# The loads and stores of 97 or 98 rows cut into 96 rows and a rest, in a graph kernel on one core

## The chip, the cores and the metric

The kernel runs on one core of a Trainium2 chip. A core has four computing engines, TensorE (PE), VectorE (DVE), ScalarE (ACT) and GpSimd (POOL), and SyncE (SP), which here issues nearly all direct transfers. The transfers run on 16 DMA engines that the core's queues share. The metric is the device time of one execution in microseconds (us); lower is better.

## The reference

There are 6250 nodes with 64 features each, and 200,000 edges sorted by their receiving node. Two layers follow each other.

```python
# layer 0: an average over the edges, weighed by the edges' own attributes
zmax = max(x, axis=-1)
q = 0.95 * zmax[src] * e[:, 1] + e[:, 0]
z_new = 0.2 * x + 0.8 * segment_sum(q, dst) / (segment_sum(e[:, 1], dst) + 1e-6)
x = layernorm(x + where(deg > 0, z_new, x))
# layer 1: four heads of attention over the same edges
s = einsum('hef,hef->eh', Q[:, dst], K[:, src]) * 64 ** -0.5
alpha = segment_softmax(s, dst)
agg = segment_sum(alpha * V[:, src], dst)      # mean over the heads
x = layernorm(x + (x + nan_to_num(agg) @ Wout))
```

## The kernel before, in words

The program has a preparation, a first edge stage (layer 0), a node update, a second edge stage (layer 1) and an end. The change touches transfers of the preparation and one store between the two edge stages.

**Preparation.** The lists `src` and `dst` are brought into SBUF as rows of RE = 2048 edges, one row on each partition: 97 full rows and a last one of 1344 edges, TP_ = 98 rows in all. SP waits for `s_init` (VectorE has cleared the last rows of `src_raw` and `dst_raw`) and then issues, in this order, `src_raw` (L287, L288), `dst_raw` (L289, L290), the node features `x` (L292 for 48 blocks of 128 nodes, L293 for the last 106 nodes) and six transfers of weights (L295 to L298). An engine issues in its program's order, so a transfer that SP can't hand over yet holds all behind it.

VectorE waits for `src_raw` (`s_sall`) and makes of it the codes `row_a`, `row_b` and `row_q` (L558 to L568), and the high part of each index (L562), which ScalarE casts (L985). SP stores the three rows of codes to `codes_dram` (L302, with two rows more at the end, L303). VectorE then waits for `dst_raw` (`s_dall`) and makes the receivers' place relative to the lowest of their chunk (L572 to L582, after which `s_rel` is set), and the table of visits (L586 to L605, then `s_vst`). SP stores that table and loads it back as one row (L310 to L315, `s_vld`).

TensorE turns four weights (L1181, once all weights are there, `s_w`), which ScalarE copies (L978 to L982) ahead of its cast of the high parts (L985). TensorE then turns the high parts (L1194), ScalarE copies them out of PSUM (L992), and only then, with `s_rel` set too, TensorE turns the relative places with the same line L1194 and the same four banks. VectorE clears `code_t` (L615) only after that (`s_relT`), and goes on with the table of node maxima (L627 to L633), the window numbers (L638 to L642) and the number of passes (L704, which needs `s_vld`), and sets `s_max`. That releases SP, PE, ACT and POOL into the first edge stage.

GpSimd makes its constants, clears the sums (`acc`, L428), waits for the stored codes (`s_coded`) and for `s_rel`, and clears `present` (L432).

**First edge stage.** 196 steps of 1024 edges: SP loads the edge attributes (L327) and the codes (L320), the other engines work in a pipeline.

**Between the stages.** ScalarE permutes the receivers (`dst_perm`, L1029, `s_dstt`), SP stores them to `dst_turned` (L373) and waits for that store (`s_dsts`) and then for the last sums (`s_all1`). The node update follows on the other engines.

**Second edge stage.** GpSimd gathers the updated nodes of 391 chunks with indirect transfers (L518); the other engines work on each chunk.

Of the kernel before, what the change touches and what calls it, by code (L numbers as in the profile page):

```python
# [14 lines left out]
CPP = 4  # L15
CH = P * CPP
# [6 lines left out]
def gnn_resnorm_kernel(nc, x, src, dst, edge, Wq, Wk, Wv, Wout, out):  # L23
    N, D = x.shape
    E = src.shape[0]
# [12 lines left out]
    FULL = E // CH  # L38
    SJ = 2 * CPP
    SC = P * SJ  # L40
    NS = -(-E // SC)
# [5 lines left out]
    W = 24  # L47
# [3 lines left out]
    SB = 3  # L51
    U2 = 48
    H2 = 7
    NCH = FULL + 1
    NC = -(-NCH // S2) * S2
    NBL = NC // S2
    EPAD = NC * CH
    TP_ = NC // CPP
    assert NS % UN == 0 and UN % S1 == 0 and UN % (4 * RQ) == 0 and 0 < TAIL <= P and (E - (NS - 1) * SC) % CPP == 0 and NC % CPP == 0
    assert NS * SC == EPAD and 2 * TP_ == NS and (NCH - H2) % U2 == 0 and NBL > SB and E - FULL * CH > 0 and (E - FULL * CH) % CPP == 0 and 2 * W <= D and NS % 4 == 0  # L60
    UG = -(-NB // 4)
    assert NB % 4 == 1
    LAST = N - (NB - 1) * P
# [2 lines left out]
    with ctx:  # L66
# [6 lines left out]
        def sem(name):  # L73
            return ctx.enter_context(nc.semaphore(name))


        dst_turned = nc.dram_tensor("dst_turned", [EPAD], F32, kind="Internal").ap()
        codes_dram = nc.dram_tensor("codes_dram", [3, EPAD + 4 * SC], BF16, kind="Internal").ap()
# [10 lines left out]
        RE = CPP * CH  # L89
        src_raw = big[0:TP_, t0:t0 + RE].bitcast(I32)  # L90
# [40 lines left out]
        dst_raw = O[0:TP_, 4 * HB:4 * HB + RE].bitcast(I32)  # L131
# [9 lines left out]
        dst_perm = big[0:TP_, t1 + RE:t1 + 2 * RE]  # L141
# [67 lines left out]
        s_dstt, s_dsts, s_x, s_w, s_dall, s_sall, s_vst, s_vld, s_codes, s_coded = (  # L209
            sem(n) for n in ("dst_turned", "dst_stored", "x_loaded", "w_loaded", "dst_all_loaded", "src_all_loaded",  # L210
                             "visits_stored", "visits_loaded", "codes_made", "codes_stored"))
# [62 lines left out]
        def blocks(g):  # L274
            return min(TB, NB - TB * g)
# [7 lines left out]
        def _(sp):  # L283

            LR = E - (TP_ - 1) * RE
            sp.wait_ge(s_init, 1)
            sp.dma_start(src_raw[0:TP_ - 1, :], src[0:(TP_ - 1) * RE].rearrange("(a b) -> a b", b=RE)).then_inc(s_sall, 16)  # L287
            sp.dma_start(src_raw[TP_ - 1:TP_, 0:LR], src[(TP_ - 1) * RE:E].rearrange("(a b) -> a b", b=LR)).then_inc(s_sall, 16)  # L288
            sp.dma_start(dst_raw[0:TP_ - 1, :], dst[0:(TP_ - 1) * RE].rearrange("(a b) -> a b", b=RE)).then_inc(s_dall, 16)  # L289
            sp.dma_start(dst_raw[TP_ - 1:TP_, 0:LR], dst[(TP_ - 1) * RE:E].rearrange("(a b) -> a b", b=LR)).then_inc(s_dall, 16)  # L290
            sp.wait_ge(s_x, 16)
            sp.dma_start(x1v[:, 0:NB - 1, :], x[0:(NB - 1) * P, :].rearrange("(b p) d -> p b d", p=P)).then_inc(s_x, 16)  # L292
            sp.dma_start(x1v[0:LAST, NB - 1, :], x[(NB - 1) * P:N, :]).then_inc(s_x, 16)  # L293
# [5 lines left out]

            def put_codes(r, t, n):  # L300
                sp.wait_ge(s_codes, n)
                sp.dma_start(codes_dram[r, 0:EPAD].rearrange("(p e) -> p e", e=RE), t[:, :]).then_inc(s_coded, 16)  # L302
                sp.dma_start(codes_dram[r, EPAD:EPAD + 4 * SC].rearrange("(p e) -> p e", e=RE), t[0:2, :]).then_inc(s_coded, 16)  # L303

            put_codes(1, row_a, 1)
            put_codes(2, row_b, 2)
            put_codes(0, row_q, 3)

            sp.wait_ge(s_vst, 1)
# [32 lines left out]
                        sp.wait_ge(b_done, pair0 + (2 * (g - RQ) + 2 + (0 if i is None else i * (UN // 2))))  # L342
                    load_rows(g + (0 if i is None else i * (UN // 4)), g % RQ)

            sp.wait_ge(s_coded, 96)
            sp.wait_ge(s_free, 1)
            sp.wait_ge(s_max, 1)
            with sp.Fori(0, sp.value_load(visits[0:1, 7 * NC:7 * NC + 1], min_val=1, max_val=300)):
# [21 lines left out]
                sp.dma_start(dst_b[b % SB], dst_turned[b * S2 * CH:(b + 1) * S2 * CH].rearrange("(a e) -> a e", a=1).broadcast_to([2 * GN, S2 * CH])).then_inc(ld2[b % SB], 16)  # L370

            sp.wait_ge(s_dstt, 1)
            sp.dma_start(dst_turned.rearrange("(p e) -> p e", e=RE), dst_perm).then_inc(s_dsts, 16)  # L373
            sp.wait_ge(s_dsts, 16)
            sp.wait_ge(s_all1, 2)
            for b in range(SB):
                load_chunks(b)
# [21 lines left out]
        def _(pool):  # L399
# [27 lines left out]
            pool.wait_ge(s_const, 7)  # L427
            pool.memset(acc, 0.0).then_inc(s_acc0, 1)  # L428
            pool.memset(ones[:, :], 1.0)
            pool.wait_ge(s_coded, 96)  # L430
            pool.wait_ge(s_rel, 1)
            pool.memset(present, 0.0).then_inc(s_pres0, 1)  # L432

# [77 lines left out]
            for c in range(NCH):  # L511
                b, k = c // S2, c % S2
# [16 lines left out]
        def _(dve):  # L529
            links = [0]  # L530

            def link(ins):

                links[0] += 1
                ins.then_inc(dch, 1)
                dve.wait_ge(dch, links[0])
# [17 lines left out]
            def lanes_first(t, h=2):  # L554
                return t.rearrange("r (h j p) -> r h j p", h=2 * h, j=CPP)

            dve.wait_ge(s_sall, 32)
            link(dve.tensor_scalar(lo_a, src_raw, 4, 7, ALU.logical_shift_right, ALU.bitwise_and))  # L558
            link(dve.tensor_scalar(lo_b, src_raw, 15, None, ALU.bitwise_and))
            link(dve.tensor_scalar(lanes_first(row_a), split(lo_a), -4.0, None, ALU.add))  # L560
# [7 lines left out]
            link(dve.tensor_tensor(row_q, row_q, sq_a, ALU.add))  # L568
            dve.sem_inc(s_codes, 1)

            dve.wait_ge(s_dall, 32)
            link(dve.tensor_copy(dst_all, dst_raw))  # L572
            link(dve.tensor_scalar(dst_low, dst_all, 0.0, float(NPAD), ALU.is_lt, ALU.mult))
            link(dve.tensor_tensor(dst_low, dst_low, dst_all, ALU.add))
# [209 lines left out]
                    invert_first(g - 3)  # L784

            link(dve.memset(U[:, NW * P:(NW + 1) * P], 0.0))
            dve.wait_ge(s_dsts, 16)
            for u in range(UG):
                if wide_of(u)[1] > 1:
                    dve.wait_ge(s_up, u + 1)  # L790
# [184 lines left out]
        def _(act):  # L975
# [78 lines left out]
            def keep_turned(u):  # L1054
                nb = wide_of(u)[1]
                rows_, n = (P, nb // 2 * P) if nb > 1 else (D, P)
                act.wait_ge(s_xT, u + 1)
                if u > 1:
                    act.wait_ge(s_up, u - 1)
                act.copy(xt1[u % 2][0:rows_, 0:n], u_turn[u % 2][0:rows_, 0:n]).then_inc(s_xTc, 1)  # L1060

            act.wait_ge(s_dsts, 16)
            keep_turned(0)
            for u in range(UG):
                if u + 1 < UG:
# [83 lines left out]
            for g in range(TG + 3):  # L1149
                for h in range(-(-blocks(g) // 2) if g < TG else 0):  # L1150
                    n = min(2, blocks(g) - 2 * h) * 2 * P
# [4 lines left out]
                if 0 <= g - 1 < TG:  # L1156
                    n = blocks(g - 1) * 2 * GN
# [6 lines left out]
                if 0 <= g - 2 < TG:  # L1164
                    k, nb = g - 2, blocks(g - 2)
# [4 lines left out]
                if 0 <= g - 3 < TG:  # L1170
                    k, nb = g - 3, blocks(g - 3)
# [298 lines left out]
```

## Time and profile before

| | |
|---|---|
| median of 3 runs | 2893.26 us (2886.39 to 2896.32) |
| the profiled execution's own time | 2893.56 us |
| its span, from the first instruction to the last | 2891.3 us |
| time outside the span | 2.3 us |
| start of the first edge stage on TensorE | 110.25 us |
| start of the first gather of the second edge stage | 819.11 us |
| mean granted TensorE clock, as a share of full speed | 0.709 |

All times within the span count from the span's start. An engine's busy time says how long it worked, and not that anything waited for it; the chain of work that ended last says what the end waited for.

### The profile page before, as it was taken

The page shows a single profiled execution, that of the slowest core. Times are in us where ns is not written, and L with a number is a line of the kernel's source. Part 1 is how long each engine was busy: PE and PEld are TensorE (multiplying, and loading weights), DVE is VectorE, ACT ScalarE, POOL GpSimd, SP SyncE. Part 2 cuts the span into 40 slices and gives each one's busy share as a digit, 9 for nine tenths or more (in the row PEclk, how much of TensorE's full clock was granted, in tenths as well). Part 3 has the DMA queues.
Part 4 walks back from the last instruction along what each step waited for, and adds up shares of the span by engine and source line. Part 5 has one row for each costly group of instructions (what it writes and reads, how often), then busy time and mean ns, then how long its engine had stood idle before and what let it go on. Part 6 is the DMA issues. An engine that isn't in the chain of part 4 may idle for free.

```text
span 2891.3 us, 78363 instructions
## 1 busy us (share of the span) xinstructions
PE 2144.7 (74%) x25183; PEld 1557.5 (54%) x25184; DVE 1768.1 (61%) x6022; ACT 1310.4 (45%) x3789; POOL 1896.0 (66%) x2644
## 2 busy tenths in 40 slices
PE   0476776666878787878877878878787877778875
PEld 0365665555746555545545555545565545555554
DVE  2676666676775655555556655655555555656568
ACT  0344333343364444444545544545444444545443
POOL 1355554455677777777777777777777777777750
PEclk9978777787675766676567666776656677776577
DMA  1455555455212122221222212222122221222111
GB/s 43 136 176 178 165 161 164 157 176 165 62 31 43 33 43 44 43 43 36 43 43 43 44 36 43 44 43 43 37 43 43 43 43 36 43 43 43 36 20 24
DMA packets 175709, 197.71 MB, mean 68 GB/s; under 512 B 95155, under 2 KB 97891, under 8 KB 173217
## 3 DMA queue, kind: packets, MB, share of 16 engines
q1 hardware_dynamic: 125030, 138.90, 16.8%
q0 software_dynamic: 50048, 51.35, 9.6%
q8 instruction: 280, 4.59, 0.7%
q14 instruction: 351, 2.88, 0.3%
HBM read 184.87 MB, written 5.25 MB: 66 GB/s over the span
## 4 chain that ended last, share of the span: by engine, by line
POOL 33%; PE 25%; issue 21%; DVE 9%; DMA 6%; SPq 3%; DVEq 1%; ACT 1%; ACTq 0%; POOLq 0%
POOL XS L518 32%; DMA XS<-x_dram,dst_bs 6%; PE psN L1234 3%; PE psS L1397 3%; PE psV L1356 3%; PE psM L1356 3%; PE psX L1225 2%; PE psM L1234 2%; PE psV L1225 2%; PE psT L1351 2%; DVE zm L685 1%; POOL XS L441 1%; DVE O L806 1%; PE psX L1346 1%; PE psN L1346 1%
## 5 line engine op out<-in xcount | busy, mean ns | idle before, releaser
L518 POOL DMA_INDIRECT XS<-x_dram,dst_bs x1564 | 1492.1, 954 | 487.9 <-issue 445.6
L803 DVE SCALAR_TENSOR_TENSOR l_st<-l_st,alpha,rsum 64x1 f32 x782 | 169.5, 217 | 552.7 <-PE psV L1356 279.7
L1397 PE MATMUL psS<-XT,Ubuf 96*128 96x512 f32 x522 | 417.1, 894 | 18.7 <-ACT Ubuf L1084 18.4
L875 DVE TENSOR_REDUCE rmax<-psS 128x1 f32<-128x512 f32 x391 | 270.2, 691 | 39.6 <-issue 16.2
L1356 PEld LDWEIGHTS psV<-XS,PT 128*128 128x128 f32 x1568 | 285.0, 271 | 1.4 <-ACT PT L1133 1.2
L1356 PE MATMUL psV<-XS,PT 128*128 128x64 f32 x1568 | 284.6, 346 | 0.7 <-ACT PT L1133 0.7
L1356 PEld LDWEIGHTS psM<-XS,dst_bs 128*128 128x128 f32 x1560 | 281.5, 270 | 1.6 <-ACT dst_bs L1133 1.6
L1356 PE MATMUL psM<-XS,dst_bs 128*128 128x64 f32 x1560 | 281.6, 345 | 0.7 <-ACT dst_bs L1133 0.7
L1133 ACT COPY PT<-psT 128x512 f32<-128x512 f32 x196 | 114.7, 585 | 349.6 <-PE psT L1351 349.0
L441 POOL TENSOR_TENSOR XS<-XS,zm 128x192 f32<-128x192 f32 x196 | 115.9, 592 | 239.1 <-DVE zm L685 237.7
L1133 ACT COPY dst_bs<-psT 128x512 f32<-128x512 f32 x195 | 114.1, 585 | 343.8 <-PE psT L1351 340.1
L1346 PEld LDWEIGHTS psX<-ident,XS 128*128 128x128 f32 x392 | 58.1, 184 | 390.1 <-issue 388.5
L1346 PEld LDWEIGHTS psN<-ident,XS 128*128 128x128 f32 x390 | 57.6, 183 | 380.8 <-issue 379.6
L1346 PE MATMUL psX<-ident,XS 128*128 128x128 f32 x392 | 108.5, 372 | 163.5 <-DMA XS<-x_dram,dst_bs 160.1
L1346 PE MATMUL psN<-ident,XS 128*128 128x128 f32 x390 | 107.1, 369 | 157.4 <-DMA XS<-x_dram,dst_bs 151.9
L1397 PE MATMUL psS<-dst_bs,Ubuf 96*128 96x512 f32 x260 | 210.0, 903 | 7.9 <-ACT Ubuf L1084 7.9
L1014 ACT ACTIVATE dst_bs<-psA,code_c 128x512 bf16<-128x512 f32 x98 | 67.3, 687 | 319.6 <-PE psT L1219 318.5
L1123 ACT ACTIVATE dst_bs<-psS,cur 128x512 f32<-128x512 f32 x195 | 134.0, 687 | 140.0 <-DVE cur L891 125.2
L1123 ACT ACTIVATE Pm<-psS,cur 128x512 f32<-128x512 f32 x196 | 134.7, 687 | 121.3 <-DVE cur L891 120.5
L797 DVE TENSOR_SCALAR XT<-big,win_ids 32x512 f32<-32x512 f32 x269 | 131.5, 489 | 73.6 <-issue 72.3
L1351 PE MATMUL psT<-ident,dst_bs 128*128 128x128 f32 x780 | 171.7, 362 | 5.1 <-ACT dst_bs L1123 4.8
L1351 PE MATMUL psT<-ident,Pm 128*128 128x128 f32 x784 | 173.1, 363 | 2.2 <-ACT Pm L1123 2.1
(276 smaller groups left out, 4408.6 us busy)
## 6 DMA issues: line engine op xcount, KB each, us to landing
big<-in_edge_attr_2x SPq DMA_DIRECT2D x195, 512.0 KB, 4.0
big<-dst_turned SPq DMA_DIRECT2D x49, 512.0 KB
XS<-x_dram,dst_bs POOLq DMA_INDIRECT x1564, 2.5
O<-codes_dram SPq DMA_DIRECT2D x200, 6.0 KB
x_dram<-x SPq DMA_DIRECT2D x12, 128.0 KB, 1.9
out<-big SPq DMA_DIRECT2D x12, 128.0 KB
codes_dram<-O SPq DMA_DIRECT2D x3, 392.0 KB
dst_turned<-big SPq DMA_DIRECT2D x1, 784.0 KB
```

Source lines behind the costliest of these rows:

```text
L441: return pool.tensor_tensor(buf[:, :, W:2 * W], buf[:, :, 0:W], z[:, :].unsqueeze(2).broadcast_to([P, SJ, W]), ALU.mult)
L518: pool.indirect_dma_start(xs(k, j), None, x1_dram, bass.IndirectOffsetOnAxis(ap=idx2[b % SB][:, k * CPP + j:k * CPP + j + 1], axis=0)).the ...
L797: dve.tensor_scalar(t[D:96, :], dst_b[J // S2 % SB][:, J % S2 * CH:(J % S2 + 1) * CH], ids, None, ALU.not_equal).then_inc(s, 1)
L803: dve.scalar_tensor_tensor(out=ls, in0=ls, scalar=al[half], in1=rs[half], op0=ALU.mult, op1=ALU.add)
L875: dve.tensor_reduce(rmax[:, q:q + 1], psSc[q][:, :], AX_X, ALU.max)
L1123: act.activation(Pms[a][:, :], psSc[a][:, :], ACT.Exp, bias=cur[:, a:a + 1], accum_out=rsum[:, a:a + 1]).then_inc(exp_done, 1)
L1133: act.copy(PTs[a][:, :], psT[:, :]).then_inc(pt_done, 1)
L1234: last = pe.matmul(ps[q * QT:(q + 1) * QT, h * 2 * W:h * 2 * W + n], e_sb[slot][:, h, c, q * QT:(q + 1) * QT], buf[:, j, 0:n], start=(c == ...
L1346: last = pe.transpose(psXc[b][:, j * P:(j + 1) * P], two, ident[:, :])
L1351: last = pe.transpose(ps[:, j * P:(j + 1) * P], probs[:, j * P:(j + 1) * P], ident[:, :])
L1356: last = pe.matmul(ps, pt[:, j * P:(j + 1) * P], xs(k, j), start=(j == 0), stop=(j == CPP - 1))
L1397: pe.matmul(psSc[1 - a][:, :], Ubuf[1 - a][:, :], XT[(J - 1) % 3][:, :], start=True, stop=True).then_inc(s_done, 1)
```

## The change

Each transfer whose partition side is 97 or 98 rows becomes one of TM = 96 rows and further ones for the rest. When the lists are loaded, the two rows of the rest are transfers of their own, each written as 16 pieces of 128 or 84 elements. When codes and `dst_turned` are stored, the two rows of the rest are one transfer written as 2 times 8 pieces of 256 elements, and so is the store of two rows behind the codes. The waits count the greater number of transfers. The stores and the load of the visits table stay as they were.

```diff
+            TM = TP_ // 16 * 16
+
+            def load_words(t, flat, done):
+                sp.dma_start(t[0:TM, :], flat[0:TM * RE].rearrange("(a b) -> a b", b=RE)).then_inc(done, 16)
+                for r in range(TM, TP_):
+                    n = RE if r < TP_ - 1 else LR
+                    sp.dma_start(t[r:r + 1, 0:n].rearrange("a (k e) -> a k e", k=16),
+                                 flat[r * RE:r * RE + n].rearrange("(a k e) -> a k e", a=1, k=16)).then_inc(done, 16)
...
-            sp.dma_start(src_raw[0:TP_ - 1, :], src[0:(TP_ - 1) * RE].rearrange("(a b) -> a b", b=RE)).then_inc(s_sall, 16)
-            sp.dma_start(src_raw[TP_ - 1:TP_, 0:LR], src[(TP_ - 1) * RE:E].rearrange("(a b) -> a b", b=LR)).then_inc(s_sall, 16)
-            sp.dma_start(dst_raw[0:TP_ - 1, :], dst[0:(TP_ - 1) * RE].rearrange("(a b) -> a b", b=RE)).then_inc(s_dall, 16)
-            sp.dma_start(dst_raw[TP_ - 1:TP_, 0:LR], dst[(TP_ - 1) * RE:E].rearrange("(a b) -> a b", b=LR)).then_inc(s_dall, 16)
+            load_words(src_raw, src, s_sall)
+            load_words(dst_raw, dst, s_dall)
...
-                sp.dma_start(codes_dram[r, 0:EPAD].rearrange("(p e) -> p e", e=RE), t[:, :]).then_inc(s_coded, 16)
-                sp.dma_start(codes_dram[r, EPAD:EPAD + 4 * SC].rearrange("(p e) -> p e", e=RE), t[0:2, :]).then_inc(s_coded, 16)
+                sp.dma_start(codes_dram[r, 0:TM * RE].rearrange("(p e) -> p e", e=RE), t[0:TM, :]).then_inc(s_coded, 16)
+                for at, rows_ in ((TM * RE, t[TM:TP_, :]), (EPAD, t[0:2, :])):
+                    sp.dma_start(codes_dram[r, at:at + 2 * RE].rearrange("(p k e) -> p k e", p=2, k=8), rows_.rearrange("p (k e) -> p k e", k=8)).then_inc(s_coded, 16)
...
-            sp.wait_ge(s_coded, 96)
+            sp.wait_ge(s_coded, 144)
...
-            sp.dma_start(dst_turned.rearrange("(p e) -> p e", e=RE), dst_perm).then_inc(s_dsts, 16)
-            sp.wait_ge(s_dsts, 16)
+            sp.dma_start(dst_turned[0:TM * RE].rearrange("(p e) -> p e", e=RE), dst_perm[0:TM, :]).then_inc(s_dsts, 16)
+            sp.dma_start(dst_turned[TM * RE:EPAD].rearrange("(p k e) -> p k e", p=2, k=8), dst_perm[TM:TP_, :].rearrange("p (k e) -> p k e", k=8)).then_inc(s_dsts, 16)
+            sp.wait_ge(s_dsts, 32)
...
-            dve.wait_ge(s_sall, 32)
+            dve.wait_ge(s_sall, 48)
```

The waits of GpSimd on `s_coded`, of VectorE on `s_dall` and of VectorE and ScalarE on `s_dsts` change in the same way.

At SP's start, the beginning of the preparation, the queue of transfers reads before (tile on the left of the arrow is written, `big` is the buffer that holds `src_raw`, `O` the one that holds `dst_raw`, the shape is rows by elements):

```order
L287 DMA big<-in_src 97x2048
L288 DMA big<-in_src 1x1344
L289 DMA O<-in_dst 97x2048
L290 DMA O<-in_dst 1x1344
L292 DMA x<-in_x 128x48x64
L293 DMA x<-in_x 106x64
L295 DMA XT<-in_L_gnn_Wq 64x4x64
```

And with the change:

```order
L289 DMA big<-in_src 96x2048
L292 DMA big<-in_src 1x2048
L292 DMA big<-in_src 1x1344
L289 DMA O<-in_dst 96x2048
L292 DMA O<-in_dst 1x2048
L292 DMA O<-in_dst 1x1344
L299 DMA x<-in_x 128x48x64
L300 DMA x<-in_x 106x64
L302 DMA XT<-in_L_gnn_Wq 64x4x64
```

Two transfers more stand ahead of `x`, and nothing has changed its place against another transfer.

Between the stages SP's queue reads before, with the store of the permuted receivers and the first loads of the second edge stage:

```order
L373 DMA dst_turned<-big 98x2048
L367 DMA dst_bs<-in_src 128x8x4
L370 DMA big<-dst_turned 32x4096
L367 DMA dst_bs<-in_src 128x8x4
L370 DMA big<-dst_turned 32x4096
```

And with the change:

```order
L381 DMA dst_turned<-big 96x2048
L382 DMA dst_turned<-big 2x2048
L375 DMA dst_bs<-in_src 128x8x4
L378 DMA big<-dst_turned 32x4096
L375 DMA dst_bs<-in_src 128x8x4
L378 DMA big<-dst_turned 32x4096
```

One transfer is added there. The instructions of the other engines are the same and in the same order.

## Rows read from the trace of the kernel before

**Rows 1.** The page: busy time by engine, and the last chain by engine.
```profile
PE 2144.7 (74%) x25183; PEld 1557.5 (54%) x25184; DVE 1768.1 (61%) x6022; ACT 1310.4 (45%) x3789; POOL 1896.0 (66%) x2644
...
POOL 33%; PE 25%; issue 21%; DVE 9%; DMA 6%; SPq 3%; DVEq 1%; ACT 1%; ACTq 0%; POOLq 0%
```

**Rows 2.** Last chain, in order of time, 0 to 130 us: start, length, what.
```profile
5.95 8.29 SPq L288
...
14.90 28.10 SPq L290
...
44.89 28.42 SPq L293
...
76.70 2.19 DMA wo<-in_L_gnn_Wout
...
82.72 1.91 ACT big L985
...
87.59 6.75 ACT O L992 x4
...
106.56 0.03 DVEq L706
...
110.25 0.58 PE psA L1219
```

**Rows 3.** Stretches (length, five engines' busy times with instructions, clock, DMA share, GB/s).
```profile
14.30:37.70 23.40, 0.00 (x0) 0.00 (x0) 0.00 (x0) 0.00 (x0) 1.26 (x2) 1.00 0.06 27
...
43.30:50.00 6.70, 0.00 (x0) 0.00 (x0) 5.91 (x5) 0.00 (x0) 0.00 (x0) 1.00 0.67 167
...
77.40:84.50 7.10, 2.14 (x16) 1.74 (x16) 6.53 (x14) 3.17 (x5) 0.02 (x1) 1.00 0.59 185
...
110.00:130.00 20.00, 13.02 (x426) 10.33 (x430) 10.72 (x27) 8.74 (x14) 8.50 (x25) 0.91 0.83 292
```

**Rows 4.** VectorE in order of time: start, length, instruction, idle before.
```profile
5.34 0.11 DVE L541 MEMSET x<- 128x64 f32 x1
...
37.70 1.23 DVE L558 TENSOR_SCALAR big<-big 98x2048 int32<-98x2048 int32 x1 [30.10 <-DMA big<-in_src]
...
48.35 1.23 DVE L568 TENSOR_TENSOR O<-O 98x2048 bf16<-98x2048 bf16 x1
70.38 1.23 DVE L572 CAST big<-O 98x2048 f32<-98x2048 int32 x1 [20.80 <-DMA O<-in_dst]
...
80.27 2.29 DVE L582 TENSOR_TENSOR big<-big,wide 98x2048 f32<-98x2048 f32 x1
...
84.52 5.35 DVE L600 TENSOR_SCALAR lohi_i<-lohi_i 98x4 int32<-98x4 int32 x1
...
90.51 0.39 DVE L605 COPY words<-lohi_i 98x4 int32<-98x4 int32 x4
...
97.52 0.17 DVE L615 MEMSET big<- 128x128 f32 x1 [5.76 <-PE psM L1194]
...
105.80 0.55 DVE L704 TENSOR_REDUCE visits<-visits 1x1 int32<-1x392 int32 x1 [0.20 <-DVE win_ids L642]
```

**Rows 5.** GpSimd, TensorE and SP in order of time, 0 to 100 us.
```profile
4.88 10.64 POOL L428 MEMSET big<- 128x12640 f32 x1
...
79.03 0.28 PE L1181 MATMUL psS<-ident,XT 64*64 64x64 f32 x1 [79.03 <-DMA wo<-in_L_gnn_Wout]
...
84.48 5.37 POOL L432 MEMSET O<- 128x6320 f32 x1 [68.92 <-DMA codes_dram<-O]
...
90.98 0.32 SPq L310 DMA_DIRECT2D visits_dram<-wide_i  x1
...
95.53 0.21 SPq L315 DMA_DIRECT2D visits<-visits_dram  x1
```

**Rows 6.** SP and GpSimd in order of time, 740 to 820 us.
```profile
745.04 0.35 SPq L373 DMA_DIRECT2D dst_turned<-big  x1
752.32 0.39 SPq L367 DMA_DIRECT2D dst_bs<-in_src  x1
...
819.11 1.17 POOL L518 DMA_INDIRECT XS<-x_dram,dst_bs  x1 [3.78 <-DMA x_dram<-x]
```

More of the change, by code:

```diff
@@ L59, in gnn_resnorm_kernel @@
     assert NS % UN == 0 and UN % S1 == 0 and UN % (4 * RQ) == 0 and 0 < TAIL <= P and (E - (NS - 1) * SC) % CPP == 0 and NC % CPP == 0
-    assert NS * SC == EPAD and 2 * TP_ == NS and (NCH - H2) % U2 == 0 and NBL > SB and E - FULL * CH > 0 and (E - FULL * CH) % CPP == 0 and 2 * W <= D and NS % 4 == 0
+    assert NS * SC == EPAD and 2 * TP_ == NS and (NCH - H2) % U2 == 0 and NBL > SB and E - FULL * CH > 0 and (E - FULL * CH) % CPP == 0 and 2 * W <= D and TP_ % 16 == 2 and NS % 4 == 0
     UG = -(-NB // 4)
@@ L429, in _ @@
             pool.memset(ones[:, :], 1.0)
-            pool.wait_ge(s_coded, 96)
+            pool.wait_ge(s_coded, 144)
             pool.wait_ge(s_rel, 1)
@@ L569, in _ @@
             dve.sem_inc(s_codes, 1)
-            dve.wait_ge(s_dall, 32)
+            dve.wait_ge(s_dall, 48)
             link(dve.tensor_copy(dst_all, dst_raw))
@@ L786, in _ @@
             link(dve.memset(U[:, NW * P:(NW + 1) * P], 0.0))
-            dve.wait_ge(s_dsts, 16)
+            dve.wait_ge(s_dsts, 32)
             for u in range(UG):
@@ L1060, in keep_turned @@
                 act.copy(xt1[u % 2][0:rows_, 0:n], u_turn[u % 2][0:rows_, 0:n]).then_inc(s_xTc, 1)
-            act.wait_ge(s_dsts, 16)
+            act.wait_ge(s_dsts, 32)
             keep_turned(0)
```

## The prediction

> **What bounds the kernel now.** I read the page's shares first, then the chain of work that ended last, then the engines in order of time around each place that the change touches. No engine is busy for more than 74% of the span, and the last chain is spread over GpSimd (33%), TensorE (25%) and gaps of issue (21%) [rows 1]. So the kernel is a row of stages, each with a bound of its own, and a change is worth what it takes from the one stage it stands in.
>
> The first stage is the preparation. TensorE starts the first edge stage at 110.25 us, and until about 77 us the chain is almost nothing but SP: 8.29 us on L288, 28.10 us on L290 and 28.42 us on L293 [rows 2]. These are not transfers, they are SP unable to hand over the next one. The stretch from 14.3 to 37.7 us says why: the DMA share is 0.06, which is one engine of 16, at 27 GB/s [rows 3]. The 97 rows of `src` (776 KB, 794,624 bytes) at 27 GB/s take 29.4 us; VectorE, which waits for them, starts at 37.70, and for `dst` at 70.38, after idling 30.10 and 20.80 us [rows 4]. The 32.7 us between these starts are once more the time of 776 KB on one engine. Other shapes do not behave so: while the 128 rows of `x` are loaded the share is 0.67 (167 GB/s), while the 98 rows of codes are stored 0.59 (185 GB/s) [rows 3]. It is the loads of 97 rows that run on one engine.
>
> After 77 us the chain goes through weights, ScalarE and TensorE: weights landed and turned at 79.03, cast L985 until 84.63, copies L992 until 94.34, the second turn L1194, and with it VectorE's L615 at 97.52, after 5.76 us of idling [rows 2, 4, 5]. From there to `s_max` at 106.56 it is VectorE alone [rows 2].
>
> **The loads of src and dst.** SP issues at 5.5 as before. Nothing in the trace shows 96 rows, so I bound their rate by the slowest and the fastest stretch in which many engines worked, 167 and 292 GB/s [rows 3], and take 2.2 us for issue to landing of a small transfer from the weights' last row [rows 2]. `src` then lands between 5.9 + 2.7 + 2.2 = 10.8 and 5.9 + 4.8 + 2.2 = 12.9 us, `dst` between 5.9 + 5.4 + 2.2 = 13.5 and 17.6. The four single rows are 8 KB or less each, below 0.4 us even on one engine.
>
> **When VectorE starts.** GpSimd clears `acc` from 4.88 to 15.52 us [rows 5]. VectorE's L600 has 4 elements per row and took 5.35 us: it began 0.04 us after GpSimd's L432, another clearing, and ended at 89.87, GpSimd's at 89.85 [rows 4, 5]. VectorE's clearing L541 ran in 0.11 us in the midst of `acc`'s [rows 4], so not every operation is held. L558 is a tensor_scalar like L600, from SBUF to SBUF. I take it that it is held to 15.52 and ends about 1.1 us later, at 16.6, wherever in 10.8 to 12.9 `src` lands; unheld it would end at 12.0 to 14.1. The choice goes by the nearest row, L600. The Trainium skill says this as a rule (SBUF — State Buffer, "Who interferes with whom"): a VectorE instruction in a two-port mode and a GpSimd instruction exclude each other for their whole length, and the one that came second waits. L600 agrees; by that rule the sum is the one below, without it 2.5 to 4.6 us more are gained.
>
> **The sum.** L558 ended at 38.93; at 16.6 it is 22.3 us earlier. L568 then ends at 49.58 - 22.3 = 27.3, and `dst` has been there since 17.6 at the latest, so the 20.80 us of idling go too: L572 starts at 27.3, 43.1 us earlier. `s_rel` comes with L582's end, 82.56 - 43.1 = 39.5. GpSimd's L432 follows at once, since codes made by 27.3 and stored in some 7 us (first issue of a store at 77.4 to L432 at 84.48 [rows 3, 5]) are there by 34.5. It holds the next tensor_scalar of VectorE as before, now L587 and not L600, until 39.6 + 5.4 = 45.0; of VectorE's small operations up to L605's end 2.7 us are left, so `s_vst` comes at 47.7 (90.90 before). The three operations up to L613 take 0.9 more: 48.6.
>
> Then comes L615, which waited. Its other side now: `x` and the weights no longer stand behind two loads on one engine. `src`, `dst` and `x` are 3.16 MB, through at 5.9 + 10.8 = 16.7 us (292 GB/s) or 5.9 + 18.9 = 24.8 us (167 GB/s); from the end of L293's wait (73.31) to the turning of the weights (79.03) it was 5.7 us [rows 2, 5], so TensorE starts at 22.4 to 30.5. From 79.03 to the end of L992 (94.34) it was 15.3 us, which gives 37.7 to 45.8. TensorE's second turn starts when this and `s_rel` (39.5) are there and takes 2.9 us (94.48 to 97.35): done at 42.6 to 48.8. VectorE arrives at 48.6. I take it that the 5.76 us wait is gone; in the worst case 0.2 us of it stay. L615 starts at 48.6 instead of 97.52: **48.9 us earlier**. What is late next: `s_vld`. The visits table went from L605's end over L310 to the load's issue at 95.53 [rows 5], and with 2.2 us to land that is 6.9 us after 90.90: at 54.6 in the new count. VectorE gets to L704 8.3 us behind L615, at 56.9. So 2.3 us of cover are left and nothing waits.
>
> **The added transfers.** Two more in SP's head cost about 0.4 us each by the median of such rows (0.35 us for L373, 0.32 for L310 [rows 5, 6]), 0.8 us ahead of `x`; they fall into the 2.9 to 6.0 us between landing and use above. Three more stores of codes, 1.2 us, come while SP has nothing to do until 47.7, and L432 has from 34.5 to 39.5 to spare. Without that cover they would cost the 1.2 us.
>
> **The store of dst_turned.** SP issues at 745.04, is through the store's wait and that of the last sums at 752.32, and the first gather starts at 819.11 [rows 6]. 98 rows or 96 and 2, at 185 GB/s 803 KB take 4.3 us; with 2.2 us that is before 752. The next consumers of what SP loads there stand 67 us later. I cost it at nothing; all of it, if uncovered, is 0.4 us.
>
> The edge stages have the same instructions and only begin earlier. Sum: 48.9 us off the profiled execution's own 2893.56 gives 2844.7; that execution is 0.3 us above the median of the runs, so I predict **2844.4 us**.
>
> **The rivals.**
> 1. *VectorE is not held by the clearing of acc.* For it: L541 ran within the clearing. Against: L600. VectorE is then 2.5 to 4.6 us earlier throughout, but L615 still needs the second turn (42.6 to 48.8, or 2 us less at the lower end), so 0 to 4.6 us are gained on top: 2840 to 2844, centre 2841.
> 2. *The other side of L615 is late.* If `x`, in its pieces of 256 bytes, runs well below 167 GB/s, L293 again holds SP and the weights. At half that rate `x` ends 9.4 us later than my upper bound, the second turn at 58.2, and the gain is 39 us: 2854. Against: 167 GB/s was the rate of `x` itself while one engine was still held by `dst`.
> 3. *96 rows run on one engine as 97 did.* The trace shows one engine for 97 rows and many for 98 and 128 rows, none for 96. The head then stays, with four small rows more: 2893 to 2894. The skill's page DMA: Bandwidth & Descriptors ("Why a DMA increments its semaphore by 16 and not by 1") says the number of engines is the largest up to 16 that divides the row count: 1 for 97, 14 for 98, 16 for 96. The rows for 97 and 98 agree; 96 no run has shown yet.
> 4. *Slower: the clock takes it back.* TensorE's chain is 25% of the span, 723 us, at a mean granted clock of 0.709. After a shorter rest the clock may be granted lower for the rest of the run. It would have to fall to 0.709 x 723 / (723 + 48.9) = 0.664 to swallow the gain, and to 0.656 for 0.3% slower, 2902 us. For it: the clock fell from 1.00 in the idle head to 0.91 as soon as the first stage began [rows 3]. Against: the rest that is lost is 2% of the span.
>
> **How the numbers follow.** The forecast has a chance of 0.62, rival 1 0.16, rival 2 0.13, rival 3 0.05, rival 4 0.04 (half of it swallowing only a part). About 0.3% (9 us) is what a measurement of this kernel can tell from no change: its three runs lie 10 us apart. That spread, about 5 us to either side, belongs on every case. The range goes from rival 1 less that, 2834, to rival 2 with some of it, 2857. Faster by over 0.3% in all cases but rival 3 and half of rival 4: 0.93; within 0.3% 0.05; slower 0.02.
>
> **What would show it.** DMA share well above 0.06 from 6 to 17 us. L558 as one long row that begins at 11 to 13 and ends at 16.6 (rival 1: a row of 1.2 us). No idle time before L572. SP's row for the last nodes of `x` under 10 us and not 28. L587, not L600, held for 5 us. L615 with next to no idle time (rival 2: a long one, released by L1194). TensorE's first L1219 at about 61.3. From there to the end 2781 us as before (2891.3 - 110.25), and a mean clock of 0.70 to 0.71. The prediction is wrong if L615 or L704 waits for more than 3 us, or if the stretch behind the head grows by more than 9 us.

## The result, and the profile after

The changed kernel took 2847.03 us in the median of 4 runs (2838.03 to 2851.35), the kernel before 2891.49 us beside it (2886.39 to 2896.32). The ratio is 0.9842 with a 95% interval of 0.9812 to 0.9872: 1.6% faster. The profiled execution took 2848.22 us with a span of 2846.0 us. Line numbers are as before up to L285; behind that L287 is now L289, L558 is L567, L615 is L624, L1219 is L1228.

The busy times by engine and the last chain, from the page, answer to [rows 1]:

```profile
PE 2170.8 (76%) x25183; PEld 1582.8 (56%) x25184; DVE 1774.2 (62%) x6022; ACT 1313.2 (46%) x3789; POOL 1901.5 (67%) x2644
...
POOL 36%; PE 24%; issue 21%; DVE 11%; DMA 6%; DVEq 1%; ACT 1%; ACTq 0%; SPq 0%; POOLq 0%
```

SP's queue, 3% of the chain before, has gone to 0%. The chain in order of time, 0 to 70 us (start, length, what), has one load, 5 us long, where [rows 2] had 65 us of SP, and from 11.39 us to 57.9 us it is VectorE alone:

```profile
5.53 0.41 SPq L289
...
6.37 5.00 DMA big<-in_src
11.36 0.02 issue
11.39 5.28 DVE big L567
...
37.34 2.30 DVE big L591
...
39.97 5.24 DVE wide L596
...
48.81 0.17 DVE big L624
...
57.86 0.03 DVEq L715
...
61.54 0.58 PE psA L1228
```

VectorE, SP, TensorE, ScalarE and GpSimd in order of time answer to [rows 4, 5]:

```profile
11.39 5.26 DVE L567 TENSOR_SCALAR big<-big 98x2048 int32<-98x2048 int32 x1 [3.79 <-DMA big<-in_src]
...
27.45 1.23 DVE L581 CAST big<-O 98x2048 f32<-98x2048 int32 x1
...
39.97 5.23 DVE L596 TENSOR_SCALAR wide<-wide 98x4 f32<-98x4 f32 x1
...
48.81 0.17 DVE L624 MEMSET big<- 128x128 f32 x1
```

```profile
8.80 10.84 SPq L300 DMA_DIRECT2D x<-in_x  x1
...
52.94 0.21 SPq L323 DMA_DIRECT2D visits<-visits_dram  x1
```

```profile
25.71 0.28 PE L1190 MATMUL psS<-ident,XT 64*64 64x64 f32 x1 [25.71 <-DMA wo<-in_L_gnn_Wout]
...
43.24 0.86 PE L1203 MATMUL psM<-ident,big 98*128 98x98 f32 x4
```

```profile
4.90 10.64 POOL L437 MEMSET big<- 128x12640 f32 x1
...
39.81 5.37 POOL L441 MEMSET O<- 128x6320 f32 x1 [24.24 <-DVEq L593]
```

The reader is to see four things. VectorE idles 3.79 us for `src` and no longer at all for `dst` or at L624, where it idled 30.10, 20.80 and 5.76 us. L567 ends at 16.65, 1.1 us after GpSimd's clearing. The second turn ends at 44.10, 4.7 us before VectorE wants it. And the loads run wide: the stretch from 5.5 to 17 us (`src`, `dst` and the first part of `x`) has a DMA share of 0.93 at 212 GB/s, where [rows 3] had 0.06 and 27 GB/s; from 7.5 to 8.5 us, when only rows of 8 KB moved, it is 0.99:

```profile
5.50:17.00 11.50, 0.00 (x0) 0.00 (x0) 6.55 (x4) 0.00 (x0) 10.07 (x2) 1.00 0.93 212
...
7.50:8.50 1.00, 0.00 (x0) 0.00 (x0) 0.10 (x1) 0.00 (x0) 1.00 (x1) 1.00 0.99 336
```

TensorE's first edge step came at 61.54 us instead of 110.25: 48.71 us earlier. From there to the end it was 2846.0 - 61.54 = 2784.5 us, against 2781.1 before. Ten profiles on chips of like speed (the two kernels and eight runs below) have 2770.6 to 2784.6 us in that stretch, without an order by kernel.

### The profile page after: what moved, and what is told of

It reads as the page before. It is cut to its first block, busy times and chain, and to the rows that moved or that the text cites. A ratio compares the mean times of both kernels' runs of the same rounds, so it can differ in the third digit from the quotient of the medians.

```text
span 2846.0 us, 78369 instructions
## 1 busy us (share of the span) xinstructions
PE 2170.8 (76%) x25183; PEld 1582.8 (56%) x25184; DVE 1774.2 (62%) x6022; ACT 1313.2 (46%) x3789; POOL 1901.5 (67%) x2644
## 4 chain that ended last, share of the span: by engine, by line
POOL 36%; PE 24%; issue 21%; DVE 11%; DMA 6%; DVEq 1%; ACT 1%; ACTq 0%; SPq 0%; POOLq 0%
POOL XS L527 35%; DMA XS<-x_dram,dst_bs 5%; PE psN L1243 3%; PE psS L1406 3%; PE psV L1365 3%; PE psM L1365 3%; PE psM L1243 2%; PE psX L1234 2%; PE psV L1234 2%; PE psT L1360 1%; DVE O L815 1%; DVE zm L694 1%; POOL XS L450 1%; PE psX L1355 1%; DVE XS L664 1%
## 5 line engine op out<-in xcount | busy, mean ns | idle before, releaser
L1406 PE MATMUL psS<-XT,Ubuf 96*128 96x512 f32 x522 | 424.2, 909 | 14.3 <-ACT Ubuf L1093 14.0
L884 DVE TENSOR_REDUCE rmax<-psS 128x1 f32<-128x512 f32 x391 | 270.5, 692 | 39.9 <-issue 19.4
L1365 PEld LDWEIGHTS psV<-XS,PT 128*128 128x128 f32 x1568 | 293.0, 278 | 1.6 <-ACT PT L1142 1.6
L1365 PE MATMUL psV<-XS,PT 128*128 128x64 f32 x1568 | 292.5, 353 | 0.7 <-ACT PT L1142 0.7
L1365 PEld LDWEIGHTS psM<-XS,dst_bs 128*128 128x128 f32 x1560 | 290.0, 277 | 2.0 <-ACT dst_bs L1142 1.5
L1365 PE MATMUL psM<-XS,dst_bs 128*128 128x64 f32 x1560 | 288.1, 350 | 0.7 <-ACT dst_bs L1142 0.7
```

Of the source, the lines that this page charges most:

```text
L884: dve.tensor_reduce(rmax[:, q:q + 1], psSc[q][:, :], AX_X, ALU.max)
L1365: last = pe.matmul(ps, pt[:, j * P:(j + 1) * P], xs(k, j), start=(j == 0), stop=(j == CPP - 1))
L1406: pe.matmul(psSc[1 - a][:, :], Ubuf[1 - a][:, :], XT[(J - 1) % 3][:, :], start=True, stop=True).then_inc(s_done, 1)
```

## The experiments

The start of TensorE's first edge step is the measure in all of them: between profiles of kernels with the same head it agrees within 0.4 us, while whole executions of one kernel scatter by 5 to 7 us to either side. A run without an interval beside it is a single execution.

**Loads alone, stores alone.** `loads_only` keeps the change of the loads and stores `codes_dram` and `dst_turned` as before:

```diff
-sp.dma_start(codes_dram[r, 0:TM * RE]..., t[0:TM, :]) ; two stores of 2 rows in pieces
+sp.dma_start(codes_dram[r, 0:EPAD]..., t[:, :]) ; one store of 2 rows
-dst_turned in 96 rows and 2
+dst_turned in 98 rows
```

> Only the loads of src and dst are cut; codes and dst_turned are stored as before. My theory, that the loads are the whole gain: VectorE's first operation on src starts at 11.4 us, TensorE's first edge step at 61.5 us as in the changed kernel, span 2846 us give or take 5. If the stores had a part in it, the clearing of present would be held up by the stored codes and the first step would come later than 62 us, or the node update would start later after the last edge step.

`stores_only` is the opposite: `load_words` gives way to the 97-row and one-row loads, the stores stay cut.

> Only the stores are cut; src and dst are loaded as 97 rows and 1. My theory: nothing is gained, first edge step at 110 us, VectorE idles some 30 and 21 us for src and dst, span 2891 us give or take 5. If the stores had a part in it: a first step earlier than 109.5 us.

Measured: the first step at 61.53 us in `loads_only` (span 2846.1) and at 110.31 in `stores_only` (span 2886.0).

```profile
61.53 0.58 PE L1226 MATMUL psA<-O,code_w 3*128 3x512 bf16 x1 [11.59 <-DMA O<-codes_dram]
```

```profile
110.31 0.58 PE L1230 MATMUL psA<-O,code_w 3*128 3x512 bf16 x1 [11.63 <-DMA O<-codes_dram]
```

The loads are the whole gain. The span of `stores_only` is 5.3 us under that before, but its head is the same; the difference lies in the stretch behind, within its spread (2775.7 us here). In the changed kernel SP's wait after the store of `dst_turned` still ended with VectorE (5.7 us, before 6.9), not with the store.

**One list alone.** `src_only` cuts `src` and loads `dst` as 97 rows and 1.

```diff
-            load_words(dst_raw, dst, s_dall)
+            sp.dma_start(dst_raw[0:TP_ - 1, :], ...)      # 97 rows
+            sp.dma_start(dst_raw[TP_ - 1:TP_, 0:LR], ...)
```

> src is cut, dst is loaded as 97 rows and 1. The theory that the queue behind a load on one engine counts as much as the load: dst lands at about 38 to 39 us, x and the weights stand behind it in that engine's queue, the weights are turned at about 47 to 48 us, the second turn ends at about 66, the VectorE clearing behind it idles some 5 us again, and the first edge step is at about 79 us. The rival, that only VectorE's own waits for src and dst count: the clearing starts at about 60.4 us without idling and the first step is at about 73 us.

```profile
43.98 1.23 DVE L582 CAST big<-O 98x2048 f32<-98x2048 int32 x1 [16.69 <-DMA O<-in_dst]
...
71.08 0.17 DVE L625 MEMSET big<- 128x128 f32 x1 [5.94 <-PE psM L1204]
```

```profile
17.04 1.23 SPq L300 DMA_DIRECT2D x<-in_x  x1
18.31 28.52 SPq L301 DMA_DIRECT2D x<-in_x  x1
```

The first step came at 83.93 us: 26.3 us of the 48.7 are gained. The mechanism is the one I named: SP stands 28.52 us at the last rows of `x`, the weights turn at 52.59, and L625 idles 5.94 us. The rival of 73 us is refuted. My number was 5 us low, because `dst` landed at 43.98 and not at 38 to 39. I had let it start at once at 27 GB/s; it stands behind the first engine's share of `src` (from 12 to 17 us it runs alone, at 26 GB/s), and by estimate that explains some 3 us of it.

**What slows the one engine.** `dst_alone` is `src_only` with SP held until `dst` has landed:

```diff
+            sp.wait_ge(s_dall, 32)
             sp.wait_ge(s_x, 16)
             sp.dma_start(x1v[:, 0:NB - 1, :], ...)
```

> As src_only, but SP waits until dst has landed before it issues x and what follows. In src_only dst landed at 43.98 us, some 2.6 us later than its bytes at 26 GB/s behind the share of src on that engine give (41.4). The theory that x, which flows meanwhile, slows the one engine: dst lands at 41 to 41.8 us here. The rival, that the load has that duration by itself: 43.7 to 44.2 us. x and the weights start then, so the first edge step comes at about 84 to 90 us in either case.

```profile
41.28 1.23 DVE L583 CAST big<-O 98x2048 f32<-98x2048 int32 x1 [14.00 <-DMA O<-in_dst]
```

```profile
17.00:30.00 13.00, 0.00 (x0) 0.00 (x0) 9.73 (x7) 0.00 (x0) 0.00 (x0) 1.00 0.06 26
30.00:41.00 11.00, 0.00 (x0) 0.00 (x0) 0.00 (x0) 0.00 (x0) 0.00 (x0) 1.00 0.06 26
```

`dst` landed at 41.28: the other 2.7 us come from `x`, which in `src_only` was issued at 17.04 us, behind `dst`, and flowed at the same time. That `dst` took longer than `src` in the kernel before too (32.7 us from landing to landing) fits. Whether `x` delays it in the engine itself or in memory, this run doesn't tell. The first edge step came at 84.90 us, within the 84 to 90 expected.

**How many engines a load gets.** `rows_94` loads 94 rows and four single rows, each of these in 16 pieces:

```diff
-                sp.dma_start(t[0:TM, :], flat[0:TM * RE]...)
-                for r in range(TM, TP_):
+                sp.dma_start(t[0:TM - 2, :], flat[0:(TM - 2) * RE]...)
+                for r in range(TM - 2, TP_):
```

> As the changed kernel, but src and dst are loaded as 94 rows and four single rows in 16 pieces. The theory that the number of engines is a divisor of the row count of at most 16 (94 = 2 x 47): two engines, 54 GB/s; src lands at about 22 us, dst at about 37, the weights are turned at about 45 and the first edge step is at about 76 us. The rival, that loads just below 97 rows spread well and 97 is special by its size or by its odd count: src lands at 11 to 12 us and the first step is at 61 to 63 us.

```profile
24.80 1.23 DVE L567 TENSOR_SCALAR big<-big 98x2048 int32<-98x2048 int32 x1 [17.20 <-DMA big<-in_src]
```

```profile
12.00:17.00 5.00, 0.00 (x0) 0.00 (x0) 0.00 (x0) 0.00 (x0) 3.56 (x2) 1.00 0.13 54
```

A share of 0.13 is two engines of 16, at 54 GB/s. So two rows fewer than 96 cost 80.90 - 61.54 = 19.4 us of the head. `src` was 2.8 us and the first step 4.9 us later than I had worked out; the share and the rate are as expected. The weights turned at 49.68 us and not at about 45, and VectorE idled 5.66 us before L624 for the second turn, which carries the lateness to the first step. Some 1.1 us for each list is an estimate for the four single rows (30 KB at 27 GB/s), if they run on one of the two engines; the rest of the landing isn't explained by a run.

`rows_97_pieces` was to tell whether the rows or the pieces decide:

```diff
-                sp.dma_start(t[0:TM, :], flat[0:TM * RE].rearrange("(a b) -> a b", b=RE))
+                sp.dma_start(t[0:TM + 1, :].rearrange("a (k e) -> a k e", k=16),
+                             flat[0:(TM + 1) * RE].rearrange("(a k e) -> a k e", k=16, e=RE // 16))
```

> As the changed kernel, but src and dst are loaded as 97 rows, each row written as 16 pieces, and one single row. The theory that the outermost count, 97, sets the number of engines: one engine still, DMA share 0.06, src lands at about 38 us or later and the first edge step is at about 110 us. The rival, that the cut into pieces is what spreads a load: DMA share above 0.5, first step at about 61.5 us.

```profile
37.73 1.23 DVE L568 TENSOR_SCALAR big<-big 98x2048 int32<-98x2048 int32 x1 [30.13 <-DMA big<-in_src]
```

```profile
17.00:30.00 13.00, 0.00 (x0) 0.00 (x0) 0.00 (x0) 0.00 (x0) 0.00 (x0) 1.00 0.06 26
```

One engine still, and the first step at 110.09. But the run doesn't test pieces, because no pieces reached the queue. The trace records the load with its operands as 97 elements of 8192 bytes, here as in `stores_only`, where the rows aren't cut: rows whose pieces lie side by side were folded back. The packets of the whole execution agree, first of `stores_only`, then of `rows_97_pieces`:

```profile
DMA packets 175725, 197.71 MB, mean 69 GB/s; under 512 B 95171, under 2 KB 97907, under 8 KB 173233
```

```profile
DMA packets 175725, 197.71 MB, mean 68 GB/s; under 512 B 95171, under 2 KB 97907, under 8 KB 173233
```

So what is shown is that writing a row as adjacent pieces changes nothing. What pieces moved as such would do, no run shows.

The same holds for the rest rows of the changed kernel. Its trace records the single rows as 1 element of 8192 or 5376 bytes and the two rows of a store as 2 elements of 4096 bytes (8192 for `dst_turned`), so its 16 and 8 pieces were never there. Only the number of packets under 512 bytes differs from the kernel before (those that differ have 4 bytes each). The queue of the direct transfers has 16 more in `stores_only`, 32 more in `loads_only`, 48 more in the changed kernel and 24 more in `rows_94`. Here are the kernel before and the changed one:

```profile
q1 hardware_dynamic: 125030, 138.90, 16.8%
```

```profile
q1 hardware_dynamic: 125078, 138.90, 17.2%
```

One such packet per transfer and engine gives just these four numbers, if 97 rows use 1 engine, 94 rows 2, 98 rows 14, 96 rows 16, and the transfers of one and two rows 1 and 2. That is a reading of counts, but a narrow one. If the number of engines were the greatest common divisor of the rows and 16, which the runs with 97, 94 and 96 rows alone would allow, 98 rows would use 2 and `stores_only` would have 64 more. If the single rows used 16 engines, `loads_only` would have 92 more.

**Is VectorE held by GpSimd?** The next three kernels and the first timing of the fourth ran on another chip, on which the kernel before took 3451.88 us; heads can be compared across chips, whole times only within one. `clear_on_act` gives the clearing of `acc` to ScalarE:

```diff
-            pool.memset(acc, 0.0).then_inc(s_acc0, 1)
...
+            act.wait_ge(s_init, 1)
+            act.mul(big[:, ta:ta + 2 * AN], code_c[:, 0:1].broadcast_to([P, 2 * AN]), 0.0).then_inc(s_acc0, 1)
```

> As the changed kernel, but ScalarE (idle until 26 us) clears the sums acc and GpSimd doesn't. The theory that GpSimd's clearing holds VectorE's first operation on src: that operation takes 1.2 us from 11.4 us instead of 5.3, all that follows is 4.0 us earlier, and the first edge step is at 57.5 us. The rival, that it is long because transfers still write the same rows or its first access is slow: it stays at 5.3 us and the first step at 61.5 us.

```profile
11.28 1.23 DVE L566 TENSOR_SCALAR big<-big 98x2048 int32<-98x2048 int32 x1 [3.68 <-DMA big<-in_src]
```

The operation takes 1.23 us instead of 5.26, while the transfers go on, and the first step is at 57.44, 4.1 us earlier. Rival 1 of the prediction, that VectorE isn't held, is refuted with that: the hold was real and cost 4.1 us. While ScalarE clears instead, VectorE isn't held.

`present_early` releases GpSimd's second clearing when the receivers are read, three operations into `dst`:

```diff
+            dve.sem_inc(s_read, 1)      # behind dst_low = dst_low + dst_all
...
-            pool.wait_ge(s_rel, 1)
+            pool.wait_ge(s_read, 1)
             pool.memset(present, 0.0).then_inc(s_pres0, 1)
```

> As the changed kernel, but GpSimd clears present as soon as the receivers have been read out of that memory (after three VectorE operations on dst) and the codes are stored, and not after s_rel. The theory: the clearing runs at about 32.4 to 37.8 us, mostly under VectorE's two reductions, which it doesn't hold; it holds the next tensor_scalar by about 0.8 us, the later one falls from 5.2 to 0.2 us, and the first edge step is at about 57.3 us. The rival, that reductions are held too or that the later one is long for another reason: first step at 61 us or later.

VectorE and GpSimd in order of time, 28 to 40 us:

```profile
32.40 2.29 DVE L586 TENSOR_REDUCE lohi<-big 98x4 f32<-98x2048 f32 x1
34.72 2.29 DVE L587 TENSOR_REDUCE lohi<-big 98x4 f32<-98x2048 f32 x1
37.04 0.78 DVE L590 TENSOR_SCALAR wide<-lohi 98x4 f32<-98x4 f32 x1
```

```profile
32.44 5.37 POOL L441 MEMSET O<- 128x6320 f32 x1 [16.86 <-DVEq L584]
```

The two reductions run within the clearing at their usual 2.29 us, the tensor_scalar behind them ends with it (37.82 and 37.81). The first step is at 57.19, 4.35 us earlier.

`x_later` moves SP's two loads of `x` behind the stores of the codes:

```diff
-            sp.wait_ge(s_x, 16)
-            sp.dma_start(x1v ...)      # both loads
...
             put_codes(0, row_q, 3)
+            sp.wait_ge(s_x, 16)
+            sp.dma_start(x1v ...)      # both loads
```

> As the changed kernel, but SP loads x behind the stores of the codes and not ahead of the weights. The weights are turned at 15 to 18 us instead of 25.7 and the copies of the high parts end 7 to 10 us earlier; x is there by about 38 us and VectorE wants it at 50.2. The theory that VectorE's own chain alone sets the start: nothing is gained, first edge step at 61.5 us. The rival, that the weights and x still bind somewhere: the first step moves by more than 0.5 us.

The weights turned at 16.91 us instead of 25.71, and the first step stayed at 61.63. So neither the weights nor `x` bind in the changed kernel; with the two runs before it this leaves VectorE's chain, and GpSimd's holds on it, to set the start.

**All three together.**

> The three before together: acc cleared on ScalarE, present cleared early, x loaded behind the codes. With the weights out of the way the two gains should add: VectorE's clearing of code_t at about 40.5 us, the second turn done at 39.4, first edge step at about 53.2 us, 8.3 us before the changed kernel; span about 2838 us, 0.981 of the kernel before. If the weights bind in spite of it, the clearing idles and the first step is at 55 us or later.

The first step came at 53.12 us and L624 at 40.41, as expected, and the ratio to the kernel before on that chip was 0.9839 (0.9811 to 0.9867), 3389.47 us in the median of 6 runs (3387.80 to 3411.77). To compare it with the changed kernel I timed both on one chip.

> The changed kernel again, beside the next one on the same chip: first edge step at 61.5 us, ratio to the kernel before 0.983 to 0.985.

> acc cleared on ScalarE, present cleared early, x loaded behind the codes, timed beside the changed kernel: first edge step at 53.1 us, 8.4 us less than the changed kernel in the head and 8.4 us in the medians, about 0.980 to 0.982 of the kernel before. The rival, that an earlier first stage gives it back later: medians within 3 us of the changed kernel's.

| | median us | ratio to before (2886.78 us) | 95% interval | first step |
|---|---|---|---|---|
| `control`, the changed kernel | 2835.25 | 0.9814 | 0.9795 to 0.9833 | 61.56 |
| `all_three_again` | 2831.49 | 0.9799 | 0.9784 to 0.9815 | 52.76 |

```profile
52.76 0.58 PE L1230 MATMUL psA<-O,code_w 3*128 3x512 bf16 x1 [11.58 <-DMA O<-codes_dram]
```

The head is 8.8 us shorter. The medians differ by 3.8 us and the intervals overlap, so that the version beats the changed kernel as a whole isn't shown; it agrees with 8.8 us gained, with half of that and with nothing. The gain of 8.4 us in the medians that I had expected was not seen, nor is the rival decided. The profiled stretches behind the head were 2773.8 and 2777.7 us, a difference smaller than the spread.

## Why the prediction was right

*What bounds the head: right.* `stores_only` and `loads_only` put all of the gain on the loads, and `src_only` shows that the queue behind a load on one engine counts beside the load itself.

*VectorE held to 15.52: right.* The first operation ended at 16.65 against 16.6 worked out, and `clear_on_act` takes the hold away. The choice between 2844 and 2841 rested on one row (L600), and the row was enough. `src` landed at 11.37, inside 10.8 to 12.9, but that was hardly put to the test: under the hold any landing up to some 15 us gives the same start of what follows.

*The chain behind it: right.* `dst`'s block at 27.45 (27.3), the hold of L596 until 45.20 (45.0), L624 at 48.81 (48.6), the first step at 61.54 (61.3). The shift of 48.71 us stands against 48.9.

*The other side of L624: right, with room.* I had bounded the weights' turn between 22.4 and 30.5 us; it was 25.71, and the second turn ended at 44.10 (42.6 to 48.8). 4.7 us of cover were left. The visits table was issued at 52.94; with 2.2 us to land (an estimate, from the weights' row) it was there by 55.1, 2 us before VectorE's 57.10. `rows_94`, with the weights at 49.68, shows the case in which the cover is gone. The loads ran at 212 GB/s, between my bounds of 167 and 292, and `x` alone at 217 (17 to 20 us), so the condition of rival 2 wasn't met. One sign was set too tight: SP's row for the last nodes of `x` was 10.84 us and not under 10.

*The stores and the added transfers: right.* Costed at nothing, and nothing in `stores_only`. The two issues of `dst_turned` took 0.33 and 0.29 us. The pieces in which the rest rows are written did nothing, as the recorded operands above show; the sum didn't need them, since it priced each single row even on one engine.

*The clock: not what decided.* The mean granted clock was 0.696 against 0.709, a little under what I had named, and the stretch behind the head grew by 3.4 us. I had overlooked that the mean must fall by itself: the head runs at 1.00 and is 48.7 us shorter, which takes off 0.005. Behind the head it is 0.697 before ((0.709 x 2891.3 - 110.25) / 2781.1) and 0.689 after. That rest of 0.008 doesn't come back on the chip of `control`: there nine executions of the kernel before have 0.703 in the mean (0.684 to 0.714) and five of the changed kernel 0.697, a difference that the shorter head gives alone. The stretch behind the head was 2773.8 us in `control`, and 2774 us is the estimate for the kernel before on that chip (2886.78 - 2.3 - 110.25). So rival 4 is not seen.

*The total.* 2844.4 us predicted, 2847.03 measured; 2835.25 on another chip, where the kernel before took 2886.78. The differences of the medians, 44.5 and 51.5 us, lie on both sides of the head's 48.7. That the total came within 2.6 us is in part luck, since executions scatter by more; the start of the first step, 61.54 against 61.3, is the agreement that counts.

The rule that the prediction takes from the Trainium skill (SBUF — State Buffer, "Who interferes with whom") was borne out in both halves: a tensor_scalar that began within GpSimd's clearing waited for its end (5.26 us in the changed kernel, 1.23 without the clearing), a reduction didn't (2.29 us with it). The rule of the Trainium skill named with rival 3 (DMA: Bandwidth & Descriptors, "Why a DMA increments its semaphore by 16 and not by 1") gives 16 engines for 96 rows, 14 for 98, 2 for 94 and 1 for 97. The shares of 0.93, 0.13 and 0.06 for 96, 94 and 97 rows agree, and so do the counts of small packets, which are also the only row of this case that tells 14 for 98 rows from another large number.

## What to carry to other kernels

When the DMA share of a stretch is 1/16 or 2/16, look at the outermost count of the transfer that runs: 96 rows, a multiple of 16, went over all engines, 97 over one and 94 over two, and the remainder can go as small transfers for about 0.3 us of issue each. Writing a row as pieces that lie side by side did nothing here; whether an edit of this kind reached the queue at all is seen in the recorded operands and in the number and size of packets, so look there before you read its time. Count what stands behind it in the same queue too: here `dst` alone on one engine still cost 22.4 us of the head. And when a wait in the head goes, look which GpSimd clearing now falls on a VectorE tensor_scalar; clear elsewhere, or under reductions.

## What the runs showed of the hardware

A transfer of rows of 8 KB on one engine ran at 26 to 27 GB/s, and took 2.7 us more, of about 30, when another load was issued behind it and flowed at the same time (`src_only` against `dst_alone`).

Three kernels and the first timing of a fourth ran on a chip on which the same program takes 19% longer (3451.88 against 2891.49 us for the kernel before), with the head and the first edge stage as on the others. Stretches of `x_later` there, and of the changed kernel (`control`) on another chip, from the first edge step to the first gather and from there to the end (length, busy times, clock, DMA share, GB/s):

```profile
61.60:751.30 689.70, 488.28 (x17905) 411.61 (x17907) 489.42 (x1314) 271.52 (x451) 380.18 (x1047) 0.79 0.50 161
751.30:3389.40 2638.10, 1889.31 (x7231) 1317.64 (x7229) 1239.67 (x4639) 1025.44 (x3323) 1485.23 (x1577) 0.60 0.14 31
```

```profile
61.60:759.20 697.60, 497.57 (x17905) 418.59 (x17907) 489.16 (x1314) 271.68 (x450) 380.22 (x1046) 0.77 0.50 159
759.20:2835.40 2076.20, 1671.18 (x7231) 1165.41 (x7231) 1236.25 (x4639) 1026.42 (x3323) 1496.92 (x1577) 0.66 0.21 40
```

From the first edge step on both kernels have the same instructions. All of the excess is in the second edge stage: 562 us more at a granted clock of 0.60 against 0.66. TensorE's busy time is 218 us longer. GpSimd's idle time before its gathers is 1054.8 us against 484.2, and 592.8 us of it end with VectorE's L815. Why the stage takes so much longer stays open.
